# Token tiles transposed by DMA as planes of 16-bit halves instead of by TensorE, in a gated cross-attention and feed-forward block

## The reference

```python
x = x + tanh(g_xattn[0]) * xattn(layernorm(x), ctx, mask, Wq, Wk, Wv, Wo)
x = x + tanh(g_ffn[0]) * ffn(layernorm(x), clip_x, clip_down, w_gate, w_up, w_down)
# xattn: 16 heads of 32, q = x Wq, softmax(q k^T / sqrt(32)) v, then Wo
# ffn: inputs and weights rounded to 8 bits with scales from their largest
# absolute values; silu(x w_gate^T) * (x w_up^T), rounded again, times w_down^T
```

## Time and profile before

| | us |
|---|---|
| median of 3 runs | 651.65 (651.65 to 651.79) |
| profiled execution | 651.6 |
| its span in the profile | 649.6 |

### The profile page before, as it was taken

The page is one execution under the profiler, slowest core; times in us unless marked ns, Lnnn a source line. Parts: engine busy times, 40 slices in busy tenths (PEclk is TensorE's granted clock), DMA queues, the critical chain, the costliest instruction groups (busy, mean ns, idle before and its releaser), DMA issues. The chain is left out here.

```text
span 649.6 us, 12819 instructions
## 1 busy us (share of the span) xinstructions
PE 629.0 (97%) x3987; PEld 478.6 (74%) x4008; DVE 505.3 (78%) x954; ACT 319.8 (49%) x488; POOL 174.5 (27%) x392
## 2 busy tenths in 40 slices
PE   8969999999999999999999997899999999899997
PEld 6769999999999999999999997444444444344544
DVE  6686878788787887888888766688888888876764
ACT  4354544445444554544544432555555554365653
POOL 7121223223232222212212111111111110047775
PEclk9999999999999999999999999899999999999999
DMA  8639111101111011011112000058465110089723
GB/s 308 189 95 318 47 28 26 49 24 48 24 29 44 25 48 25 28 52 62 29 47 68 18 7 0 18 174 192 161 210 202 31 28 17 0 291 413 292 105 128
DMA packets 59861, 63.32 MB, mean 97 GB/s; under 512 B 39571, under 2 KB 42029, under 8 KB 59821
## 3 DMA queue, kind: packets, MB, share of 16 engines
q1 hardware_dynamic: 54915, 46.03, 23.7%
q10 hardware_dynamic: 4906, 16.78, 7.0%
HBM read 32.48 MB, written 21.36 MB: 83 GB/s over the span
## 5 line engine op out<-in xcount | busy, mean ns | idle before, releaser
L633 DVE TENSOR_REDUCE sb_smax<-ps_s 128x8 f32<-128x616 f32 x64 | 51.1, 799 | 59.4 <-PE ps_s L926 59.0
L1231 ACT ACTIVATE sb_silu<-ps_g,sb_sgu 128x512 f32<-128x512 f32 x88 | 60.5, 687 | 72.1 <-PE ps_g L1318 43.8
L1318 PE MATMUL ps_g<-sb_xqT,sb_wgu 128*128 128x512 bf16 x344 | 89.3, 379 | 1.0 <-DVE sb_xqT L1274 0.6
L1318 PE MATMUL ps_u<-sb_xqT,sb_wgu 128*128 128x512 bf16 x346 | 89.4, 379 | 0.3
L527 ACT COPY sb_pT<-ps_p 128x512 f32<-128x512 f32 (+1 forms) x96 | 46.5, 520 | 71.5 <-PE ps_p L937 71.5
L1289 DVE SCALAR_TENSOR_TENSOR sb_h<-ps_u,sb_sgu,sb_silu 128x512 f32<-128x512 f32 (+1 forms) x88 | 66.1, 751 | 19.4 <-PE ps_u L1318 18.8
L948 PE MATMUL ps_o<-sb_vblk,sb_pT 128*128 (+4 forms) x640 | 79.0, 270 | 1.2 <-ACT sb_pT L527 1.2
L948 PEld LDWEIGHTS ps_o<-sb_vblk,sb_pT 128*128 128x128 f32 (+1 forms) x640 | 76.8, 191 | 1.8 <-ACT sb_pT L527 1.4
L881 PE MATMUL ps_q<-sb_xT_hi,sb_wq_hi 128*128 128x256 f32 x256 | 78.0, 305 | 0.0
L882 PE MATMUL ps_q<-sb_xT_lo,sb_wq_hi 128*128 128x256 f32 x256 | 72.6, 284 | 0.0
L883 PE MATMUL ps_q<-sb_xT_hi,sb_wq_lo 128*128 128x256 f32 x256 | 72.6, 284 | 0.0
(11 more groups left out here) (212 smaller groups left out, 1351.8 us busy)
## 6 DMA issues: line engine op xcount, KB each, us to landing
h_spill<-sb_h SPq DMA_DIRECT2D x4, 2816.0 KB, 8.9
sb_h<-h_spill ACTq DMA_DIRECT2D x16, 704.0 KB, 7.5
out_dram<-sb_wgu SPq DMA_DIRECT2D x31, 256.0 KB, 2.1
sb_x<-in_x_dram ACTq DMA_DIRECT2D x1, 4096.0 KB, 16.8
sb_w_in<-in_L_ffn_w_gate_dram SPq DMA_DIRECT2D x11, 256.0 KB, 2.6
sb_w_in<-in_L_ffn_w_up_dram SPq DMA_DIRECT2D x11, 256.0 KB, 2.6
sb_x<-in_x_dram SPq DMA_DIRECT2D x2, 1024.0 KB, 14.7
sb_x<-in_x_dram SPq DMA_DIRECT2D x2, 512.0 KB, 5.3
```

What stands on the lines that cost most here:

```text
L633: dve.tensor_reduce(smax[:, half, :].rearrange("p (g h) -> p g h", g=2), half_scores(), X, ALU.max).then_inc(v_max, 1)
L1231: act.activation(silu[(j * KI + i) % 2][:, :, :].rearrange("p t n -> p (t n)"), p_g[(j * KI + i) % 2][:, :], ACT.Silu, scale=sgu[:, i:i + ...
L1318: last = pe.matmul(banks[(j * KI + i) % 2][:, :], wgu[:, what, k, i * P:(i + 1) * P], xqT[j][:, k, :], start=(k == 0), stop=(k == KD - 1))
```

## The change

For tile 8 and later (`DIRECT = 8`) TensorE no longer transposes the normalised tile. The fp32 tile in `xn`, seen as 1024 16-bit halves per partition, goes through these steps:

- GpSimd copies it into `xpl` as two planes, all first halves and then all second halves (`x_split`), inside the deviation of the next tile: between its second short operation and the power. It waits for `xn` to be written and for the low part of the previous tile.
- SP issues one DMA transpose of eight 128x128 blocks of 16-bit values from `xpl` back into `xn` (`planes_transposed`).
- ScalarE joins the planes into `xpl` as fp32 again (`x_join`), and copies the high part from there. The next normalisation waits for the join, as it overwrites `xn`. VectorE's low part reads `xpl` instead of `p_x`.

The SBUF array of `xabs` made room for `xpl`. The absolute values now go to the PSUM bank `p_y` for tiles before 24, and to `xpl` from tile 24 on (`PLANES_FREE = NT - 4`). So ScalarE waits there for VectorE's addition out of `p_y` (`v_x1`), and `project` of tile n-2 waits until the absolute values of tile n-4 have been reduced (`v_xmax`). VectorE's reduction is moved ahead of the second `scores_sub`, and the aggregate of the statistics (`stats_end`) ahead of the low part of x. `out_transpose` waits no longer for the low part of tiles beyond 7.

The core of the diff:

```diff
+                    def planes_transposed(n):
+                        sp.wait_ge(g_xpl, n - DIRECT + 1)
+                        sp.dma_start_transpose(xn_u[:, :].rearrange("p (c n) -> p c n", n=P),
+                                               xpl_u[:, :]).then_inc(d_xT, 16)
...
                     for w in range(2, NW):
                         rows_transposed(w - 2)
+                        if w + 3 >= DIRECT:
+                            planes_transposed(w + 3)
                         rows(w)
...
+                    def x_split():
+                        pool.tensor_copy(xpl_planes, xn_pairs).then_inc(g_xpl, 1)
...
-                        wait(pool, a_xn, n - 1)
+                        if split:
+                            wait(pool, a_xn, n)
+                            wait(pool, v_xlo, n - 1)
+                        else:
+                            wait(pool, a_xn, n - 1)
                         pool.tensor_tensor(ve[:, :], mv[:, 1:2], eps[:, :], ALU.add).then_inc(g_self, 1)
                         pool.tensor_tensor(nmean[:, :], mv[:, 0:1], minus[:, :], ALU.mult).then_inc(g_self, 1)
+                        if split:
+                            x_split()
...
+                    def x_join(n, t):
+                        wait(act, d_xT, (n - DIRECT) * 16 + 16)
+                        act.copy(xpl_pairs, xn_planes).then_inc(a_xpl, 1)
+                        wait(act, a_xpl, n - DIRECT + 1)
+                        wait(act, t_q, n - t % 2 - 2)
+                        act.copy(xT_hi[t // 2][:, :, t % 2 * P:(t % 2 + 1) * P], xpl_T).then_inc(a_xhi, 1)
...
+                                if isinstance(n, int) and n >= PLANES_FREE:
+                                    act.wait_ge(v_xlo, NT)
+                                else:
+                                    wait(act, v_x1, n - 2)
+                                act.activation(xabs(n - 4), row(n - 4), ACT.Abs, bias=nb2[:, span(n - 4)],
...
-                        dve.tensor_tensor(xT_lo[t // 2][:, :, cols], p_x[:, :, :],
+                        dve.tensor_tensor(xT_lo[t // 2][:, :, cols], xpl_T if joined(n) else p_x[:, :, :],
...
+                        if runs(n - 4, NT):
+                            wait(dve, a_abs, n - 3)
+                            dve.tensor_reduce(xmax[:, span(n - 4)], xabs(n - 4), X, ALU.max).then_inc(v_xmax, 1)
                         if runs(n, NT):
                             scores_sub(n, t, 1)
...
                         wait(pe, v_x1, m)
+                        if not isinstance(m, int) or m < PLANES_FREE - 2:
+                            wait(pe, v_xmax, m)
...
-                        if runs(n + 4, NT):
+                        if not joined(n + 4):
                             wait(pe, v_olo, n - 1)
                             x_transpose(n + 4)
```

More of the change, by code:

```diff
@@ L172, in flamingo_block, with xabs @@
                 p_y = pb("y", [P, D])
+                xn_pairs = xn_u[:, :].rearrange("p (n two) -> p two n", two=2)
+                xn_planes = xn_u[:, :].rearrange("p (two n) -> p two n", two=2)
+                xpl_planes = xpl_u[:, :].rearrange("p (two n) -> p two n", two=2)
+                xpl_pairs = xpl_u[:, :].rearrange("p (n two) -> p two n", two=2)
+                xpl_T = xpl[:, :].rearrange("p (k n) -> p k n", k=KD)
+                def xabs(m):
+                    return xpl[:, :] if isinstance(m, int) and m >= PLANES_FREE - 4 else p_y[:, :]
                 LATE = NT - 2 * (KC + KD)
@@ L308, in wait, with joined @@
                         eng.wait_ge(sem_, value)
+                def joined(n):
+                    return not isinstance(n, int) or n >= DIRECT
                 def last_tile(m):
@@ L422, in _, with deviation @@
                 def _(pool):
-                    def deviation(n, t):
+                    def x_split():
+                        pool.tensor_copy(xpl_planes, xn_pairs).then_inc(g_xpl, 1)
+                    def deviation(n, t, split=False):
                         mv, rs, nb = mv1[t % 2], rs1[t % 2], nb1[t % 2]
@@ L449, in slot @@
                         if runs(n + 5, NT):
-                            deviation(n + 5, t + 5)
+                            deviation(n + 5, t + 5, split=joined(n + 4))
+                        elif runs(n + 4, NT):
+                            wait(pool, a_xn, n + 5)
+                            wait(pool, v_xlo, n + 4)
+                            x_split()
                         if runs(n - 3, NT):
@@ L495, in normalise @@
                         wait(act, g_nb, n + 1)
-                        wait(act, t_x, n)
+                        if isinstance(n, int) and n <= DIRECT:
+                            wait(act, t_x, n)
+                        else:
+                            wait(act, a_xpl, n - DIRECT)
                         act.activation(xn[:, :], x1[:, span(n), :].rearrange("p a d -> p (a d)"), ACT.Identity,
@@ L521, in slot @@
                                 wait(act, v_xmax, n - 3)
-                                act.activation(xabs[:, :], row(n - 4), ACT.Abs, bias=nb2[:, span(n - 4)],
+                                if isinstance(n, int) and n >= PLANES_FREE:
+                                    act.wait_ge(v_xlo, NT)
+                                else:
+                                    wait(act, v_x1, n - 2)
+                                act.activation(xabs(n - 4), row(n - 4), ACT.Abs, bias=nb2[:, span(n - 4)],
                                                scale=rs2[:, span(n - 4)]).then_inc(a_abs, 1)
@@ L535, in slot @@
                         if runs(n + 4, NT):
-                            x_part(n + 4, t)
+                            if joined(n + 4):
+                                x_join(n + 4, t)
+                            else:
+                                x_part(n + 4, t)
                         if runs(n + 5, NT):
@@ L798, in slot @@
                             stats(n + 6)
+                        if runs(n + 6, NT):
+                            wait(dve, v_bn, n + 7)
+                            wait(dve, g_nb, n + 5)
                         if runs(n - 1, NT):
@@ L965, in out_transpose @@
                         if isinstance(m, int):
-                            wait(pe, v_xlo, min(m + 6, NT))
-                            wait(pe, v_olo, m)
-                        else:
-                            wait(pe, v_xlo, m + 6)
+                            wait(pe, v_xlo, min(m + 6, DIRECT))
+                        else:
+                            pe.wait_ge(v_xlo, DIRECT)
+                        wait(pe, v_olo, m)
                         for k in range(KD):
```

28 lines of the change are left out of this document (18 added, 10 removed).

## The result

| | before | after |
|---|---|---|
| median, us | 651.65 (651.43 to 651.79) | 642.69 (641.59 to 643.5) |
| ratio, with its 95% interval | | 0.986 (0.9845 to 0.9879) |
| profiled execution, us | 651.6 | 643.5 |
| its span, us | 649.6 | 641.7 |
| the core's mean granted clock | 0.994 | 0.989 |

A forecast was written before the change was run, and what follows sets the result against it. The prediction took TensorE to bound the attention slots (11.50 us each). Removing its transposes saves 24 x 0.38 = 9.1 us, with added work hidden: 651.6 - 9.1 = 642.5 us, range 640.5 to 652.0.

The forecast's parts named there:

- TensorE's transposes: Attention slots 4 to 27: removing four transposes a slot saves 0.38 us each, 24 x 0.38 = 9.1 us.
- The three readings of the cost: Four transposes a slot on TensorE: 1.09 us by durations (0.45 by load starts), 0.39 by stretch, 0.37 by whole slot.
- The projection's wait: TensorE's projection waits for VectorE's reduction of absolute values: margin 0.6 us, cost nothing; a few tenths less in slots 22 to 27.
- The join: ScalarE's copy of 1024 halves into every second place: 1.04 us, upper end 2.1, leaving ScalarE 1.2 us of margin.
- The margin beyond it: After ScalarE's 1.2 us, 0.35 more before the probabilities' copies are late; from 1.55 us lateness costs TensorE one for one.
- Split and plane transpose: GpSimd's split 1.04 us, upper end 3.4; DMA transpose landing after 3.2 us, ends 2.5 and 5.0; both hidden.
- rival A: The ring or ScalarE becomes the bound: at 12.3 us a slot 19 us slower, 671; chance 0.16.
- The ring: Normalise, split, transpose, join, high part on one buffer pair: 7.1 us a round against 11.1 a slot, four in hand.
- The sum: Whole kernel: 651.6 - 9.1 = 642.5 us, with the first stage up to slot 3, last slots and feed-forward stages untouched.
- B: Part of the gain goes into new waits of the projection or ScalarE, 0.2 us a slot: 647.3 us; chance 0.12.
- C: TensorE's transposes were free, filling gaps that stay, slots still 11.5 us: 651.6 us; chance 0.04.
- D: The transposes' full durations come back, 24 x 1.09 = 26.2 us: 625.4 us; chance 0.02.

The follow-up runs named there:

- experiment 1: Changed kernel with four unread TensorE transposes put back into each of slots 4 to 27, DMA way kept: 651.47 us, ratio 1.000.
- experiment 4: Changed kernel with ScalarE's join done twice in each slot: 658.23 us, ratio 1.010.
- Experiments 5 to 7: Changed kernel with one, three and five extra GpSimd additions of 512 fp32 columns ahead of each split but the last: 642.64, 646.79 and 684.87 us.
- experiment 9: The changed kernel run once more, unaltered: 642.9 us, ratio 0.988.
- experiment 5: Changed kernel with one extra GpSimd addition of 512 fp32 columns ahead of each split but the last: 642.64 us, ratio 0.987.
- experiments 4, 6 and 10: In order: changed kernel with join twice, 658.23 us; with three extra GpSimd additions per split, 646.79; kernel before with unread matmuls in the gaps between stages, 651.43.

## Why the prediction was right, step by step

**TensorE's transposes: right.** 0.38 us a slot were predicted, 0.39 measured; experiment 1 shows that they are the whole gain. The three readings of the cost (stretch between neighbours, whole slot, duration) differed by nearly three, and the stretch and the slot, at 0.39 and 0.37, were the right ones; the starts of the four weight loads themselves gave 0.45, a little too much. The Trainium skill, TensorE: Matmul & The Clock Gate, Part 4: PE-mode transpose, gives about 275 ns a transpose of 128x128, for bf16; the trace agrees with it as a duration for fp32 (273 ns). As a saving each of the 96 was worth 9.30 / 96 = 0.097 us.

**The projection's wait: right.** The reduction ends at 201.01, the projection's weight load follows in the timeline of after:

```profile
200.32 0.69 DVE L841 TENSOR_REDUCE sb_xmax<-ps_y 128x512 f32 x1
201.66 0.19 PEld L946 LDWEIGHTS ps_y<-sb_wo_hi,sb_oT_hi 128*128 128x128 f32 x1
```

Margin 0.65 us, predicted 0.6; in slots 22 to 27 it is 0.46 to 0.52, the few tenths less that were expected with w_down in between.

**The join: mis-sized.** 1.04 us were predicted, 1.35 measured; the bounds held it (upper 2.1). ScalarE in slot 14 and its next slot, after:

```profile
191.27 1.35 ACT L558 COPY sb_xpl<-sb_xn 128x1024 uint16<-128x1024 uint16 x1
192.65 0.62 ACT L561 CAST sb_xT_hi<-sb_xpl 128x512 fp32r<-128x512 f32 x1
193.17 0.81 ACT L548 ACTIVATE sb_xn<-sb_x,sb_nb,sb_rs 128x512 f32 x1
194.94 0.58 ACT L573 CAST sb_oT_hi<-ps_x 128x512 fp32r<-128x512 f32 x1 [0.95 <-PE ps_x L1036]
202.37 1.35 ACT L558 COPY sb_xpl<-sb_xn 128x1024 uint16<-128x1024 uint16 x1
```

The margin before the high part of the outputs is 0.95 us, predicted 1.2; VectorE's before the row maximum is 0.51, predicted 0.8. Both are short by the 0.3 us of the join. The margin absorbed it, so the sum did not move.

**The margin beyond it: wrong in its mechanism, without effect here.** The step "from 1.55 us on ScalarE's lateness costs TensorE one for one" looked only at the way from ScalarE to the probabilities and from there to TensorE. The nearer limit is the loop of VectorE and ScalarE that experiment 4 found: 10.45 us, in hand 0.65. With the join at its upper end of 2.1 us, 0.75 more than measured, the slot would by this loop have been about 11.20 us and not untouched (an estimate from its parts in experiment 4). The prediction had named VectorE's margin of 0.8 us, but not that its row maximum closes a loop, by which lateness comes back from slot to slot instead of ending in a wait.

**Split and plane transpose: right.** The groups of after, and the issues of the plane transpose (last number: median us to landing), against the earlier trace rows:

```profile
L459 POOL COPY sb_xpl<-sb_xn 128x1024 uint16<-128x1024 uint16 x24 | 24.9, 1036 | 5.1 <-DVE sb_xT_lo L676 5.1
```

```profile
sb_xn<-sb_xpl SPq DMA_TRANSPOSE x24, 3.1
```

1.04 us predicted and measured for the split. The forecast was worked out from casts without gaps, so gaps on GpSimd's 16-bit reads cost nothing beyond it; a copy without gaps was not run there. For the landing 3.2 us were predicted and 3.1 measured. The interpolation between four and eleven blocks was enough; the landing of 9.3 us in the earlier trace rows, which spoke for rival A, did not recur (longest 3.7).

**The ring: right.** From the join at 191.27 to the landing at 195.55 + 3.1 = 198.65 one round takes 7.4 us, predicted 7.1 (the 0.3 is the join's again). The next join comes at 202.37: 3.7 us in hand, predicted 4. Experiments 5 to 7 put the point from which the ring decides between 10.7 and 13.0 us, as the prediction's account has it.

**The sum: right, and nearer than its parts.** It had 9.1 us from the slots, where 9.3 came. It had the later stages untouched, and these gave 1.3 us back in the profiled execution, by a dip of the clock that goes with the absence of the transposes in most executions, though not in all (experiment 9). From 651.6 to 643.5 us the profiled execution gained 8.1 us. By the medians the gain is 9.0 us, since the profiled execution is the longest of the four (641.6 to 643.5); the second comparison of the same kernels, in experiment 9, has 651.11 against 642.9, a gain of 8.2. That the forecast met the median within 0.2 us is in part luck; the mechanism and a gain of 8 to 9 us are not. Rivals A, B, C and D would have left ScalarE waiting on the transpose, a wait of the projection, slots of 11.5, and slots of 10.4; none is in the trace. (For B the prediction had VectorE busy for over four fifths of a slot; the three windows of the earlier trace rows give 76 to 83%.)

**Open** is what decides whether the clock falls at that border. It fell and stayed in kernels whose work around the gap is the same and whose gap has the same length and, in experiment 5, a start only 0.15 us earlier. The transposes, which end some 200 us ahead of the gap, have to do with how often it falls, by the counts of experiment 9, but nothing in the records of TensorE shows how.

## What to carry to other kernels

Where TensorE is the bound of a pipeline, price what is taken from it by the starts of the neighbouring instructions or by two slots that differ in just that work; a sum of durations was nearly three times too high here. Latency that replaces it (here split, DMA and join, 7.4 us) is free as long as each ring of buffers and waits goes round within the slot. So add up every loop, those too that close over two engines and not over the buffer: the one with the least room here (0.65 us, against 3.7 in the ring) was the one that the prediction had not added up. And where a gain is near 1% of the time, look at the granted clock of each execution, stage by stage: here its falls moved the time by 1.3 to 1.6 us each, in stages that the change does not touch.

## What the runs showed of the hardware

- ScalarE copied 1024 16-bit values in 1.03 us without gaps, in 1.16 with gaps of one place on the read, in 1.35 with gaps on the write. GpSimd did the split, with gaps on the read, in 1.04 us.
- On GpSimd an addition of 512 fp32 columns with the same tile as both inputs took 1.04 us (1.09 to 1.10 each in a row of three or five). The addition of two different tiles in the earlier trace rows, which writes over one of them, took 1.72; which of the differences counts was not tested.
- A DMA transpose of eight 128x128 blocks of 16 bits, SBUF to SBUF, landed 3.0 to 3.7 us after its issue, median 3.1.
- The same gap of 1.8 us on TensorE was followed by a granted clock of 1.00 in five profiles and by a fall of it in six (to 0.50, the 1.2 GHz level, in the changed kernel), at a cost of 1.3 us there. A difference of a single profile of 0.2% may be no more than that.
- The fall behind the longer gap of 4.1 to 4.4 us (attention to up) lay before the first product of up in the kernel before and in the changed kernel. In three profiles (experiments 4, 6 and 10) it reached into up (0.57 to 0.64 in the first 4 us), and up took 152.2 to 152.5 us instead of 150.8 or 150.9.
- Without TensorE's transposes 23 of 29 executions had a mean clock of 0.991 or less, with them 1 of 72.
